# Expert rows with 16 places, lighter norm heads, and the first attention batch begun beside the last expert tiles: one core of a Trainium2 chip

## The reference

```python
x = L0_attn_x                                   # (16, 256, 256) float32: 4096 tokens of 256
x = x + 0.5 * ffn(layernorm(x), ...)
x = x + attn(layernorm(x), ...)
x = x + 0.5 * ffn(layernorm(x), ...)

def ffn(x):                                     # 16 experts, 2 per token, I = 128
    p = sigmoid(x @ gate_w.T); p = p / p.sum(-1)
    w, idx = top_k(p, 2); w = w / w.sum(-1)
    for each expert e: y[e] = (silu(x @ gate[e]) * (x @ up[e])) @ down[e]
    return sum of the two chosen y, weighted by w

def attn(x):                                    # 16 heads of 16, sequence 256, causal
    q, k, v = split(x @ w_qkv); softmax(q k^T / 4 + mask) v, then @ w_out
```

## Time and profile before

| | |
|---|---|
| median of 3 runs | 855.49 us |
| profiled execution, own time | 858.55 us |
| its span | 856.8 us |
| busy: PE, DVE, ACT, POOL | 78%, 65%, 39%, 46% |
| chain that ended last, by engine | PE 64%, DVE 12%, POOL 9%, DMA 6%, issue 5% |
| mean granted TensorE clock | 0.881 of full speed |

### The profile page before, as it was taken

The page is one execution under the profiler, slowest core; times in us unless marked ns, Lnnn a source line. Parts: engine busy times, 40 slices in busy tenths (PEclk is TensorE's granted clock), DMA queues, the critical chain, the costliest instruction groups (busy, mean ns, idle before and its releaser), DMA issues.

```text
span 856.8 us, 17032 instructions
## 1 busy us (share of the span) xinstructions
PE 669.7 (78%) x5016; PEld 516.6 (60%) x5017; DVE 558.1 (65%) x1486; ACT 330.7 (39%) x817; POOL 398.4 (46%) x466
## 2 busy tenths in 40 slices
PE   2706999999278999999999999977337999978300
PEld 1404888888155777777777777645226888856200
DVE  7598455555448888888888887636693555545443
ACT  2500334433124665555555565555302433422100
POOL 4102555554542554554444432233005755577775
PEclk9855999999679999999999999998756999988855
DMA  7680455558363444444444433203103655555754
GB/s 246 214 277 22 140 162 162 160 161 144 92 179 98 123 127 120 128 133 122 113 117 128 118 90 89 57 3 133 65 0 92 179 161 162 156 158 149 226 151 135
DMA packets 94136, 113.37 MB, mean 132 GB/s; under 512 B 11632, under 2 KB 84608, under 8 KB 94080
## 3 DMA queue, kind: packets, MB, share of 16 engines
q1 hardware_dynamic: 80224, 74.87, 28.3%
q0 software_dynamic: 13824, 37.77, 17.7%
q10 hardware_dynamic: 32, 0.02, 0.0%
HBM read 49.30 MB, written 33.55 MB: 97 GB/s over the span
## 4 chain that ended last, share of the span: by engine, by line
PE 64%; DVE 12%; POOL 9%; DMA 6%; issue 5%; ACT 2%; SPq 1%; DVEq 0%; POOLq 0%; ACTq 0%
PE bank L802 14%; PE bank L813 7%; PE bank L376 6%; POOL shared L660 6%; PE bank L435 6%; PE bank L396 5%; PE bank L421 5%; PE bank L795 4%; PE bank L383 3%; PE bank L399 3%; PE bank L455 3%; DMA shared<-normed,source 2%; PE bank L808 2%; DMA normed<-shared 2%; POOL shared L649 2%
## 5 line engine op out<-in xcount | busy, mean ns | idle before, releaser
L649 POOL DMA_INDIRECT shared<-normed,source x160 | 153.3, 958 | 191.0 <-DVE source L1084 102.5
L802 PE MATMUL bank<-wgu_sb,xeT 128*128 x640 | 171.5, 392 | 0.0
L330 POOL TENSOR_SCALAR_AFFINE_SELECT pr<-pr 128x512 f32<-128x512 f32 x128 | 81.2, 657 | 156.6 <-ACT pr L500 156.3
L551 DVE TENSOR_REDUCE mx<-bank 128x2 f32<-128x512 f32 (+1 forms) x192 | 127.0, 685 | 25.1 <-PE bank L399 22.0
L1098 DVE COPY hidT<-bank 128x128 f32<-128x128 f32 x160 | 46.6, 291 | 123.0 <-PE bank L808 122.7
L896 ACT COPY xeT<-bank 128x256 f32<-128x256 f32 x160 | 59.6, 372 | 169.9 <-PE bank L795 169.5
L802 PEld LDWEIGHTS bank<-wgu_sb,xeT 128*128 128x128 f32 x640 | 113.4, 197 | 9.3
L500 ACT ACTIVATE pr<-bank 128x512 f32<-128x512 f32 x192 | 102.8, 608 | 31.8 <-PE bank L421 19.7
L813 PE MATMUL bank<-wd_sb,hidT 128*128 x320 | 96.8, 385 | 0.7 <-DVE hidT L1098 0.7
L318 POOL DMA_INDIRECT gathered_rows<-grouped_out,slot x64 | 68.8, 1075 | 27.4 <-DMA grouped_out<-shared 13.1
L795 PE MATMUL bank<-ident,shared 128*128 128x128 f32 x320 | 64.4, 284 | 19.9 <-DMA shared<-normed,source 19.8
(11 more groups left out here) (162 smaller groups left out, 1070.0 us busy)
## 6 DMA issues: line engine op xcount, KB each, us to landing
grouped_out<-shared SPq DMA_DIRECT2D x160, 128.0 KB
shared<-parts SPq DMA_DIRECT2D x154, 128.0 KB, 2.4
spare<-parts SPq DMA_DIRECT2D x70, 128.0 KB, 2.4
normed<-shared SPq DMA_DIRECT2D x16, 512.0 KB, 3.2
x_sb<-in_L_attn_x_dram SPq DMA_DIRECT2D x4, 1024.0 KB, 9.3
wgu_sb<-_L_ffn_gate_up_proj_dram SPq DMA_DIRECT2D x8, 512.0 KB, 8.9
out_dram<-x_sb SPq DMA_DIRECT2D x16, 256.0 KB, 3.1
shared<-normed,source POOLq DMA_INDIRECT x160, 2.9
```

The costliest lines, as they stand in the source:

```text
L330: nc.gpsimd.affine_select(out=m, in_=m, compare_op=ALU.is_ge, fill=0.0, base=0, pattern=[[0, 4], [1, P]], channel_multiplier=-1).then_inc( ...
L551: nc.vector.tensor_reduce(mx[:, u, h0:h0 + nh], bank[3 + n % 2][:, :].rearrange("p (h k) -> p h k", h=nh), AX.X, ALU.max).then_inc(at["max ...
L649: nc.gpsimd.indirect_dma_start(xe[f][:, r, :], None, normed, bass.IndirectOffsetOnAxis(source[:, j:j + 1], 0)).then_inc(xe_loaded[r], 16)
L802: last = nc.tensor.matmul(bank[2 + u][:, 0:2 * I], xeT[:, u, c, :], wgu_sb[:, e, c, :], start=(c == 0), stop=(c == HC - 1))
```

## The change

Four things:

- Heads of both feed-forwards: three row buffers (BACK) instead of two; TensorE transposes two tiles into one bank, so that ScalarE copies 128x512 at once; VectorE also computes offset = -mean * rstd by groups (`shifts`). For f = 0 (`mine` = 3) the fourth row of each round is normalised by ScalarE (`normalise_last`), for f = 1 by VectorE as before. The row stores are written out, not in a loop. The area behind `slot_t` is shifted by `gap`.
- f = 1 has 16 places for expert rows (AHEAD = (4, 16)): 66 fetches stand ahead of the first result gather, VectorE's combine loop begins at expert tile 64, TensorE's loop holds 16 tiles. For both f TensorE's code is 4 tiles written out, the loop, and the rest.
- The gathers of attention's batch 0 stand between fetch 71 and fetch 72 of f = 0, its root behind fetch 79, then the gathers of batch 1. VectorE's mix, moments and norm of batch 0 stand in its last round of expert tiles. Waits for the last results are put in front of the first Q product and the first stacking DMAs.
- The conversion of the query and key weights on ScalarE stands behind the first sigmoid, no longer at attention's start.

```diff
-    AHEAD = (RING, 2 * RING)
+    AHEAD = (RING, 4 * RING)
     NK = NE_T // RING
     LOADS = 4
     LATE = 4
+    ROUNDS = NT // RING
+    BACK = 3
+    mine = (RING - 1, RING)
...
-        rows = shared[:, 5 * NT * E:5 * NT * E + 2 * RING * H].rearrange("p (i r h) -> p i r h", i=2, r=RING)
+        rows = shared[:, 5 * NT * E:5 * NT * E + BACK * RING * H].rearrange("p (i r h) -> p i r h", i=BACK, r=RING)
...
+        def attn_fetch(pool, b):
+
+            for n in range(2 * TOPK):
+                attn_gather(pool, b, n)
+
+        def attn_gather(pool, b, n):
+
+            t, j = b * 2 + n // TOPK, n % TOPK
+            r = t % RING
+            if j == 0:
+                after(pool, at["mixed"], t - RING + 1)
+            results = grouped_out[0:DONE * P, :] if t < EARLY else grouped_out
+            nc.gpsimd.indirect_dma_start(got[r][j], None, results, bass.IndirectOffsetOnAxis(slot[:, t, j:j + 1], 0))\
+                .then_inc(at[f"gathered{r}"], 16)
+
+        def attn_root(pool, b):
+
+            pool.wait_ge(at["var_ready"], b + 1)
+            ts = slice(2 * b, 2 * b + 2)
+            nc.gpsimd.tensor_tensor(rstd[:, ts], var[:, ts], minus_half[:, 0:2], ALU.pow).then_inc(at["rstd_ready"], 1)
...
+                if kind == FETCH and b > 1:
+                    if 2 * b == EARLY and n == 0:
+                        for r in range(RING):
+                            pool.wait_ge(ye_stored[r], stores(0, NE_T))
+                    attn_gather(pool, b, n)
+                if kind == ROOT and b > 0:
+                    attn_root(pool, b)
...
+                        for r in range(RING):
+                            sp.wait_ge(ye_stored[r], stores(0, NE_T))
...
+                        if b == 0:
+                            pe.wait_ge(ffn[0]["ye_ready"], NE_T)
...
+            batches(DVE_TURN, lambda kind, n, b: None if b == 0 and kind in (MIX, MOMENTS, NORM) else attn_part(dve, kind, n, b))
...
-                for j in range(NE_T):
+                for j in range(NE_T - 2 * RING):
                     fetch(j)
-                stored_up_to(NE_T)
+                stored_up_to(DONE)
+                attn_fetch(pool, 0)
+                for j in range(NE_T - 2 * RING, NE_T):
+                    fetch(j)
+                attn_root(pool, 0)
+                attn_fetch(pool, 1)
...
-                    pe.wait_ge(s["xn_ready"], k * RING + r + 1)
-                    later(pe, s["xnT_ready"], k, RING, r - RING + 1)
+                    if r < mine[f]:
+                        pe.wait_ge(s["xn_ready"], k * mine[f] + r + 1)
+                    else:
+                        pe.wait_ge(s["last_ready"], k + 1)
+                    if k > 1 and r % 2 == 0:
+                        pe.wait_ge(s["xnT_ready"], (k - 2) * 2 + r // 2 + 1)
                     for c in range(HC):
-                        last = nc.tensor.transpose(bank[r][:, c * P:(c + 1) * P], rows[:, i, r, c * P:(c + 1) * P], ident[:, :])
+                        last = nc.tensor.transpose(bank[k % 2 * 2 + r // 2][:, r % 2 * H + c * P:r % 2 * H + (c + 1) * P],
+                                                   rows[:, k % BACK, r, c * P:(c + 1) * P], ident[:, :])
                     last.then_inc(s["xn_transposed"], 1)
...
-            bodies = NE_T // body
+            alone = 4
+            loops = (NE_T - alone - 1) // body
...
-            steps(0, range(body))
-            with pe.Fori(1, bodies - 1) as k:
-                steps(k, range(body))
-            steps(bodies - 1, range(body + 2))
+            steps(0, range(alone))
+            with pe.Fori(0, loops) as m:
+                steps(m, range(alone, alone + body))
+            steps(loops, range(alone, NE_T + 2 - loops * body))
...
-                    act.wait_ge(s["xn_transposed"], k * RING + r + 1)
+                for r in range(0, RING, 2):
+                    act.wait_ge(s["xn_transposed"], k * RING + r + 2)
                     later(act, s["logitsT_done"], k, 1, -1)
-                    nc.scalar.copy(xnT[:, i, r, :, :].rearrange("p c n -> p (c n)"), bank[r][:, 0:H]).then_inc(s["xnT_ready"], 1)
+                    nc.scalar.copy(xnT[:, i, r:r + 2, :, :].rearrange("p r c n -> p (r c n)"), bank[i * 2 + r // 2][:, :])\
+                        .then_inc(s["xnT_ready"], 1)
...
+            def normalise_last(k):
+
+                act.wait_ge(s["shift_ready"], k * RING // (NT // LOADS) + 1)
+                later(act, s["xn_transposed"], k - BACK + 1, RING, 0)
+                if k >= BACK:
+                    act.wait_ge(xn_stored[k % BACK], kept(f, k % BACK, k // BACK))
+                t = k * RING + RING - 1
+                nc.scalar.activation(rows[:, k % BACK, RING - 1, :], x_sb[:, t, :], ACT.Identity, scale=rstd[:, t:t + 1],
+                                     bias=offset[:, t:t + 1]).then_inc(s["last_ready"], 1)
+
             nc.scalar.preload_act_table(ACT.Sigmoid)
+            if mine[f] < RING:
+                normalise_last(0)
             for k in range(NT // RING):
+                if k + 1 < ROUNDS and mine[f] < RING:
+                    normalise_last(k + 1)
...
+            if f == 0:
+                act.wait_ge(wqk_loaded, 16)
+                for x in range(2):
+                    for c in range(HC):
+                        nc.scalar.activation(wqk[:, c, x, :, :].rearrange("p e (d h) -> p e d h", d=D),
+                                             wqk_in[:, c, x * H:(x + 1) * H].rearrange("p (h e d) -> p e d h", e=2, d=D),
+                                             ACT.Copy, scale=1.0 if x else 1.0 / float(D) ** 0.5).then_inc(at["wqk_ready"], 1)
...
+            def shifts(c):
+                ts = slice(c * per, (c + 1) * per)
+                dve.wait_ge(s["rstd_ready"], c + 1)
+                nc.vector.scalar_tensor_tensor(out=offset[:, ts], in0=mean[:, ts], scalar=-1.0, in1=rstd[:, ts],
+                                               op0=ALU.mult, op1=ALU.mult).then_inc(s["shift_ready"], 1)
+
             def normalised(k):
-
-                later(dve, s["xn_transposed"], k, RING, -RING)
-                later(dve, s["xn_stored"][k % 2], k // 2, 16, 0)
-                for r in range(RING):
-                    normalise(rows[:, k % 2, r, :], k * RING + r).then_inc(s["xn_ready"], 1)
+                later(dve, s["xn_transposed"], k - BACK + 1, RING, 0)
+                if k >= BACK:
+                    dve.wait_ge(xn_stored[k % BACK], kept(f, k % BACK, k // BACK))
+                for r in range(mine[f]):
+                    normalise(rows[:, k % BACK, r, :], k * RING + r).then_inc(s["xn_ready"], 1)
...
-                expert_round(NK - 1, range(RING + 2))
+                expert_round(NK - 1, range(1))
+                attn_part(dve, MIX, 0, 0)
+                expert_round(NK - 1, range(1, 2))
+                attn_part(dve, MOMENTS, 0, 0)
+                expert_round(NK - 1, range(2, RING))
+                attn_part(dve, NORM, 0, 0)
+                expert_round(NK - 1, range(RING, RING + 2))
```

215 lines of the change are left out of this document (99 added, 116 removed).

## The result

The changed kernel took 827.28 us (median of 4 runs, 827.01 to 832.47) against 855.31 us for the kernel before on the same chip (855.03 to 856.14): a ratio of 0.968 [0.965, 0.971]. Its profiled execution took 827.29 us, so it stands at the median, where that of before stood 3.2 us above its own. The two profiled executions are 31.3 us apart; the medians 28.0.

What follows compares the result with a forecast made beforehand. Five stages in a row, each ended by another resource. The terms -3.0 - 8.5 - 4.3 - 6.3 = -22.1 us took the profiled 858.55 to 836.5, and the median, 3.1 lower, to 833.4; range 825 to 843.

Steps and rivals of the forecast that it cites:

- First head: First feed-forward's norm and routing logits, to the first sigmoid: ScalarE takes one row in four, third buffer; -3.0 us.
- Four gathers: Last expert tiles of the first feed-forward: four attention gathers ahead of a fetch make the experts end 2.9 us later.
- The fill: Between first feed-forward and attention's first score: earlier batch 0 work gives -8.5 us, with the four gathers' 2.9 inside.
- Rival B: Fill: batch 0's residue isn't held up, so -12 to -14.5 us and a time of about 829; chance 0.13.
- Attention: Attention's steady part: touched by no edit, TensorE busy 260.03 of 261 us, so left at its length.
- Second head: Second feed-forward's head, to the second sigmoid: third buffer and paired copies, TensorE at 1.8 us a round; -4.3 us.
- Second feed-forward: Stage to the last gather: eight gathers fewer -10.4, new combine wait +4.3, small terms -0.5 and +0.3; -6.3 us.
- the 3.1 us that I took off: Whole kernel: the runs' median stands 3.1 us below the profiled execution, turning the forecast of 836.5 into 833.4.
- A: Second feed-forward's 16-tile loop: three jumps back cost 1.7 us each and the wait grows; 838.5 us, chance 0.14.
- D: Second feed-forward's 16-tile body: code loading falls behind, each tile takes longer, the sign turns; 860 us at 0.42; chance 0.03.
- C: Both heads: stores queue and TensorE's clock drops, so -2 instead of -7.3 us, time 838.7; chance 0.14.
- E: Whole kernel: late gathers, the combine wait and heads giving nothing cancel the changes, within 0.2%; chance 0.02.

Runs made afterwards that it cites:

- its repeat: The changed kernel, nothing edited, run again on a chip where the kernel before takes 891.6 us: 884.09 us, ratio 0.992.
- the two held versions: Changed kernel, first combine at tile 56, GpSimd held to four tiles ahead for 48 fetches; with 16 places 835.09 us, with 8 places 834.28 us.
- the repeat of before: The kernel before, unchanged, profiled once more on a chip where it takes 887.0 us: 888.17 us, ratio 1.000.
- the first comparison: The first measurement of the changed kernel against the kernel before on one chip: 827.28 against 855.31 us, ratio 0.968.

## Why the prediction was right, and where it was off

I forecast 833.4 (825 to 843), and 827.28 lies in the range, 6.1 below. The waits and orders came as described; the sizes erred all in one direction, each stage but the four gathers giving more than its term.

**First head**, -3.0 against -5.0. The mechanism was right, the sizes a little too large at three places: the third group's offset let ScalarE start at 25.82, not 26.8; a round took 1.60, not 1.8; and from the last copies to the sigmoid it took 1.8 (33.55 to 35.31), not 2.5. The round came out near for mixed reasons: from start to start its norm row holds ScalarE for 0.51 us (I had 0.33), the two copies for 0.94 (1.2) and the logits copy for 0.16 (0.27). The recorded steps add up to 37.7, not 37.5, and that is -2.6, not the -3.0 taken.

**Four gathers**, +2.9 against +3.9 at the hid product of tile 79 (214.81, where 215.94 less the head's gain is 210.9). The gathers themselves cost what I took. Tile 71, just ahead of them, starts 6.1 us earlier than before (193.71 against 199.80); from there the fetch behind the gathers is 4.6 us late (I had 5.0) and tile 72 is 2.9 us late. What I left out is the clock behind the gap: it fell to the 1.2 GHz level (mean 0.58 in 198 to 202; L828 takes 0.63 us for its two matmuls at 201.25 and 0.38 at 193.71), and tiles 72 and 73 took 5.0 us instead of 3.26. That makes 4.7 us at tile 74 and 5.0 at the hid product of tile 79; 1.1 of them are hidden in the 3.9, because tile 71 was ahead by 6.1 and not by the head's 5.0 alone. The step that was mis-sized is this one: the sum had no term for the clock.

**The fill**, -8.5 against -9.2, the gathers inside. Nearly step by step: root 0 came where I had it once the head's 5.0 are taken off (218.9 less 5.0; 213.88), though the last tiles were later than forecast; first residue 12.2 us after root 0 (forecast 12.7), 12.7 from it to the score (12.6). Rival B, that the residue isn't held up, is out: it waited for the norm of batch 1.

**Attention**, 0 against -2.9. I left it at its length and should not have: at its two ends TensorE ran part of the time at the 1.2 GHz level before, and in the changed kernel at the full 2.4 throughout. The 29 us behind the first score, before and after:

```profile
253.00:282.00 29.00, 25.89 (x199) 17.58 (x200) 23.64 (x48) 13.17 (x25) 9.15 (x13) 0.87 0.43 115
```
```profile
239.00:268.00 29.00, 24.23 (x216) 16.28 (x216) 24.86 (x53) 13.15 (x26) 10.34 (x14) 1.00 0.48 131
```

and a window at attention's end, before and, at about the same work, after:

```profile
540.00:556.00 16.00, 14.39 (x122) 10.31 (x121) 9.49 (x22) 6.76 (x15) 2.81 (x5) 0.89 0.19 51
```
```profile
520.00:536.00 16.00, 14.30 (x144) 10.34 (x144) 11.06 (x24) 8.30 (x20) 3.17 (x6) 1.00 0.29 77
```

In the fill the mean clock rose as well, from 0.68 to 0.77:

```profile
217.00:239.00 22.00, 15.10 (x54) 11.50 (x54) 10.51 (x28) 5.57 (x10) 15.29 (x17) 0.77 0.69 191
```

It is not a safe gain: from root 1 to the first root of the second head the changed kernel took 342.2 us here, 343.8 in its repeat (clock 0.88 behind the first score, 1.00 at the end), and 345.8 and 345.7 in the two held versions (0.82 and 0.89), which have the same code up to there, against 347.4 and 346.4 before. What decides whether the clock falls there is not shown.

**Second head**, -4.3 against -5.2: 1.7 us a round, not 1.8, and 3.47 instead of 3.74 behind the last transposes. The recorded steps (603.7 instead of 608.28) give -4.6.

**Second feed-forward**, -6.3 against -9.3. Eight steps of 1.30 less are -10.4, the new wait is +4.6 above the usual 0.30 (I had 4.3). Another -2.5 in the gathers was in no term: the 1.70 us gap of before at 810.25 did not come back, and the average step is 1.285, not 1.30. And 1.0 lies ahead of the first result gather, where tile 8 starts 15.9 us after the first fetch instead of 16.8. Why the gap and this 1.0 went is open; the gap stands in the repeat of before too, so it is none of the 3.1 us that I took off as one execution's excess.

**Rivals.** A and D, the longer body: no tile of the jumps starts late, TensorE is busy 50.00 of 50 us. The Trainium skill (Runtime: NRT & Kernel Launch, Instruction fetch mechanics) would allow a stall at each jump out of the code held; this trace shows none at 16 tiles. C, the heads don't give: they gave 10.2 us, 2.9 more than forecast. E is out. What none of them had is what came true on the slow kind of chip: that the third part loses, because a longer fill takes back the gathers it saves and the wait of the later combine grows. I had asked for each queue what stands behind it, but not what a longer row of transfers does to the others.

## What stays open

Why the engines stand still on three chips and not on the others. Shown: the stretches come when gathers are issued in a row ahead of TensorE, at the eleventh, in either feed-forward, with 8 or 16 places and not with 4; they last longer with 16; they come again when result gathers and fetches alternate. Not shown: whether it is the number outstanding, their rate, or the semaphore traffic of their landings, and whether the recording of an execution has a part in it, since updates are missing from the records of these very chips and no time here comes without a record. The two versions that might have told drew a chip of the other kind.

The parts of the change were undone one by one only on the slow kind of chip; for the first kind the heads and the start rest on the stages of two profiles, and the places on the comparison with the held version, which differs from a plain 8-place version by that hold and was not run on the same chip beside the changed kernel.

Besides the changed kernel only the two held versions ran on a chip of the first kind, and neither beats it. On the slow kind two versions do, at 0.979 and 0.982 of before against 0.992: the first combine at tile 56, or 8 places.

## What to carry to other kernels

When a deeper buffer lets an engine run ahead, its gain comes only from what is ready when the bound moves to that engine (4.5 to 7 us of this stage here), and on the slow kind of chip the other engines stood still during the burst; measure on more than one chip before calling it a gain. A wait that a reordering adds is priced by what it is on a good day (4.86 us) and by what a delay upstream makes of it (17.77 us). When an edit shortens or opens gaps of TensorE, look at its clock in the stages next to them: here it gave some 3 us at attention's ends and took 1.8 behind the four gathers, and the first did not repeat in full.

## What the runs showed of the hardware

- Chips differ by kind. The same kernel took 855 us in the first comparison and on one chip of the experiments, and 887 to 892 on three others. In the one of these where the kernel before was profiled, all of the difference lies in the stage with long rows of indirect DMAs (240.0 us against 209.2). In the traces of the slow ones about a third of the semaphore updates is missing (10,330 of 15,724 left).
- GpSimd issues an indirect gather of 128x256 every 1.26 us, 0.96 us of it busy; a memset of 0.22 us between two lengthens that to 1.35 only.
- A norm row on ScalarE (128x256, with scale and bias) takes 0.60 to 0.67 us, on VectorE 0.34; the next instruction on ScalarE starts 0.51 us after it.
- Behind a gap of 2.8 us ahead of tile 72 the granted clock of TensorE fell to its lower level, and two expert tiles took 5.0 us instead of 3.26.
